# LayerNorm statistics and normalisation of a retention kernel: variance taken around the mean, and both tiles of a pair normalised on VectorE

## What is computed

```python
xn = _layernorm(x, axis=-1)                      # (x - mean) / sqrt(var + eps), over 1024
Q, K, V = xn@Wq+bq, xn@Wk+bk, xn@Wv+bv           # 16 heads of 64
retained = ((Q@K.T)/8 * decay_mask) @ V          # per head, decay 0.99**(i-j) for j <= i
s = (layernorm(retained)*gamma+beta) * sigmoid(xn@Wg+bg) @ Wo + bo
g = silu(gelu(xn@w1+b1) @ w2 + b2)
x = x + s * g
```

## Time and profile before

| | |
|---|---|
| median of two runs | 1882.03 us (1881.09 and 1882.97) |
| the profiled execution | 1881.47 us |
| its slowest core (core 1) | span 1879.9 us |
| spans of all cores | 1870.0 to 1879.9 us |
| mean granted TensorE clock | 0.815 to 0.817 of full speed on every core |
| busy, core 1 | PE 1335.6 us (71%), DVE 450.6 us (24%), ACT 383.8 us (20%), POOL 146.4 us (8%) |

### The profile page before, as it was taken

One profiled execution on the slowest core, in us unless ns is written; L12 is line 12 of the kernel. 1 busy time (PEld: TensorE's weight loads), 2 busy tenths in 40 slices (PEclk: granted clock), 3 DMA queues, 4 the chain that ended last, 5 costly groups with the idle time before them and its releaser, 6 DMA issues.

```text
span 1879.9 us, 21563 instructions; the slowest of 8 cores (1870.0 to 1879.9 us)
## 1 busy us (share of the span) xinstructions
PE 1335.6 (71%) x7562; PEld 708.9 (38%) x7562; DVE 450.6 (24%) x1264; ACT 383.8 (20%) x758; POOL 146.4 (8%) x144
## 2 busy tenths in 40 slices
PE   0266386685736786668757767877569999999994
PEld 0022032352322332333324323343136666666662
DVE  0413420133302522332324233242401011110011
ACT  1443203112012012021120120201012222221221
POOL 0000000000100100100100001001101122211222
PEclk9987598686865867768758767787679999999997
DMA  7201203399950000000000000004250121111110
GB/s 144 85 29 66 68 0 67 75 126 113 119 83 23 0 23 23 12 12 23 23 23 1 24 0 1 23 1 157 79 202 12 57 68 68 46 37 54 68 68 34
DMA packets 15905, 100.46 MB, mean 53 GB/s; under 512 B 3253, under 2 KB 3638, under 8 KB 11830
## 3 DMA queue, kind: packets, MB, share of 16 engines
q0 software_dynamic: 6144, 44.06, 13.6%
q1 hardware_dynamic: 9510, 46.62, 7.6%
q10 hardware_dynamic: 144, 8.39, 1.2%
HBM read 109.56 MB, written 33.55 MB: 76 GB/s over the span
## 4 chain that ended last, share of the span: by engine, by line
PE 63%; DVE 10%; DMA 9%; ACT 8%; issue 7%; POOL 2%; DVEq 0%; ACTq 0%; SPq 0%; POOLq 0%
PE pY L1043 12%; PE pH L1019 9%; PE pPJ L527 6%; PE pM L829 5%; PE pPJ L489 4%; DMA xg<-xpre 3%; PE pS L756 3%; PE pPJ L506 3%; PE pPJ L564 3%; DMA s_scr<-WB 3%; PE pLATE L663 2%; ACT xnb L358 2%; PE pRT L608 2%; PE pRT L622 2%; PE pSCB L581 2%
## 5 line engine op out<-in xcount | busy, mean ns | idle before, releaser
L1019 PE MATMUL pH<-xnT,WB 128*128 128x256 bf16 x2048 | 229.5, 274 | 11.7 <-ACT hT L1029 10.8
L1043 PE MATMUL pY<-WB,hT 128*128 128x512 bf16 x1024 | 226.2, 382 | 13.7 <-DMA WB<-w2b 13.7
L1019 PEld LDWEIGHTS pH<-xnT,WB 128*128 128x128 bf16 x2048 | 200.2, 98 | 42.6 <-issue 16.9
L756 PE MATMUL pS<-WB 128*128 128x512 bf16 x256 | 103.6, 526 | 120.0 <-POOL WB L746 66.5
L1043 PEld LDWEIGHTS pY<-WB,hT 128*128 128x128 bf16 x1024 | 100.8, 98 | 133.2 <-issue 17.2
L1029 ACT ACTIVATE hT<-pH,b1Ts 128x256 bf16<-128x256 f32 x256 | 99.7, 480 | 223.5 <-PE pH L1019 223.4
L1073 DVE SCALAR_TENSOR_TENSOR xg<-pY,xg 128x1024 f32<-128x1024 f32 x16 | 19.6, 1224 | 470.1 <-ACT xg L1070 428.1
L527 PE MATMUL pPJ<-xnT,WB 128*128 128x256 bf16 x1024 | 122.8, 283 | 12.5 <-DVE WB L518 12.3
L806 PE MATMUL pMR<-WB,cpreB 128*1 128x512 bf16 x48 | 23.9, 600 | 150.7 <-DVE WB L430 94.8
L593 DVE TENSOR_TENSOR WB<-pSCB,maskS 128x256 bf16<-128x256 f32 x128 | 54.3, 424 | 302.3 <-PE pSCA L587 296.3
L527 PEld LDWEIGHTS pPJ<-xnT,WB 128*128 128x128 bf16 x1024 | 96.8, 101 | 40.3 <-issue 16.5
(11 more groups left out here) (133 smaller groups left out, 1470.5 us busy)
## 6 DMA issues: line engine op xcount, KB each, us to landing
xg<-xpre SPq DMA_DIRECT2D x12, 1024.0 KB, 4.9
xg<-xseg SPq DMA_DIRECT2D x8, 1024.0 KB, 4.8
w1b<-w POOLq DMA_DIRECT2D x1, 8192.0 KB, 108.2
w2b<-w POOLq DMA_DIRECT2D x1, 8192.0 KB, 182.4
s_scr<-WB POOLq DMA_DIRECT2D x16, 512.0 KB, 3.0
xg<-xseg SPq DMA_DIRECT2D x16, 512.0 KB, 5.0
sld<-s_scr SPq DMA_DIRECT2D x16, 512.0 KB, 3.7
out<-sld POOLq DMA_DIRECT2D x16, 512.0 KB, 3.0
```

Of the source, the lines that this page charges most:

```text
L756: A("tensor", lambda e, it=it, dt=dt, ns=ns: e.matmul(pS[:, :], AsS[:, GRP * dt + 128 * it:GRP * dt + 128 * it + 128], WoS(1024 * dt + 512 ...
L1019: A("tensor", lambda e, dht=dht, dm=dm, sub=sub, pH=pH, gc=gc: e.matmul(pH[:, 256 * sub:256 * sub + 256], w1S(4096 * dm + 128 * dht, 128), ...
L1043: A("tensor", lambda e, lt=lt, dht=dht, ns=ns, it=it, pY=pY, half=half: e.matmul(pY[:, 512 * ns:512 * ns + 512], hT[:, 256 * lt + 128 * it ...
```

## The change

- `ln_stats` gets the negative mean between its two ACT passes: Copy with sum on ACT, then `nmu` for this one column on DVE, then Square with sum on ACT with `nmu` as its bias. What is summed is the squared distance from the mean.
- `ln_nr` loses the mean, its square, and the subtraction; mean, scale and eps become one operation. It has 16 operations instead of 19.
- `ln_finish` has one form: the DVE operation over the tile, for both tiles. The product `nbc` and the ACT operation L440 are gone.

The loops and stages that call the helpers are as before. The core of the diff (where lines are left out, lists of names for the waits are written differently):

```diff
             A("scalar", lambda e: e.activation(
                 xnb[:, :], xbuf[:, :], AF.Copy,
                 accum_out=nsum[:, cs[0]:cs[1]]),
               reads=[xtok], writes=["b.xnb", "b.nsum.%d" % sx])
-            A("scalar", lambda e: e.activation(
-                xnb[:, :], xbuf[:, :], AF.Square,
-                accum_out=v1c[:, cs[0]:cs[1]]),
-              reads=[xtok], writes=["b.xnb", "b.v1c.%d" % sx])
...
             A("vector", lambda e: e.tensor_scalar(
                 nmu[:, cs[0]:cs[1]], nsum[:, cs[0]:cs[1]], -1.0 / DM, None,
                 ALU.mult),
-              reads=_sxs("b.nsum", c0, ncols), writes=rm)
-            A("vector", lambda e: e.tensor_tensor(
-                nrT[:, cs[0]:cs[1]], nmu[:, cs[0]:cs[1]], nmu[:, cs[0]:cs[1]],
-                ALU.mult), reads=rm, writes=rt)
-            A("vector", lambda e: e.scalar_tensor_tensor(
-                vpe[:, cs[0]:cs[1]], v1c[:, cs[0]:cs[1]], 1.0 / DM,
-                nrT[:, cs[0]:cs[1]], ALU.mult, ALU.subtract),
-              reads=_sxs("b.v1c", c0, ncols) + rt, writes=rv)
+              reads=["b.nsum.%d" % sx], writes=["b.nmu.%d" % sx])
+            A("scalar", lambda e: e.activation(
+                xnb[:, :], xbuf[:, :], AF.Square, bias=nmu[:, cs[0]:cs[1]],
+                accum_out=v1c[:, cs[0]:cs[1]]),
+              reads=[xtok, "b.nmu.%d" % sx], writes=["b.xnb", "b.v1c.%d" % sx])
+
+        def ln_nr(c0, ncols):
+            cs = (c0, c0 + ncols)
+            sx = c0 // 2
             A("vector", lambda e: e.tensor_scalar(
-                vpe[:, cs[0]:cs[1]], vpe[:, cs[0]:cs[1]], EPS, None, ALU.add),
-              reads=rv, writes=rv)
+                vpe[:, cs[0]:cs[1]], v1c[:, cs[0]:cs[1]], 1.0 / DM, EPS,
+                ALU.mult, ALU.add),
+              reads=["b.v1c.%d" % sx], writes=["b.vpe.%d" % sx])
...
-            if eng == "vector":
-                A("vector", lambda e, rstd_ap=rstd_ap: e.tensor_scalar(
-                    out_ap, xbuf[:, :], nmu[:, cs[0]:cs[1]],
-                    rstd_ap[:, cs[0]:cs[1]], ALU.add, ALU.mult),
-                  reads=[xtok, "b.nmu.%d" % sx, rstd_tok] + list(extra),
-                  writes=[out_tok])
-                return
-            A("vector", lambda e, rstd_ap=rstd_ap: e.tensor_tensor(
-                nbc[:, cs[0]:cs[1]], nmu[:, cs[0]:cs[1]], rstd_ap[:, cs[0]:cs[1]],
-                ALU.mult),
-              reads=["b.nmu.%d" % sx, rstd_tok], writes=["b.nbc.%d" % sx])
-            A("scalar", lambda e, rstd_ap=rstd_ap: e.activation(
-                out_ap, xbuf[:, :], AF.Identity, bias=nbc[:, cs[0]:cs[1]],
-                scale=rstd_ap[:, cs[0]:cs[1]]),
-              reads=[xtok, "b.nbc.%d" % sx, rstd_tok] + list(extra),
+            A("vector", lambda e: e.tensor_scalar(
+                out_ap, xbuf[:, :], nmu[:, cs[0]:cs[1]], rstd_ap[:, cs[0]:cs[1]],
+                ALU.add, ALU.mult),
+              reads=[xtok, "b.nmu.%d" % sx, rstd_tok] + list(extra),
               writes=[out_tok])
...
-                    ln_finish(xb, xtok, t, xnb[:, :], "b.xnb",
-                              eng=("vector" if t == 0 else "scalar"))
+                    ln_finish(xb, xtok, t, xnb[:, :], "b.xnb")
...
-                                  scale_col=(cpreS[:, jt:jt + 1], "r.cpre"),
-                                  eng=("vector" if t2 == 0 else "scalar"))
+                                  scale_col=(cpreS[:, jt:jt + 1], "r.cpre"))
```

More of the change, by code:

```diff
@@ L289, in build_nc @@
         nrT = SB("nrT", [128, 4], F32)
-        nbc = SB("nbc", [128, 4], F32)
     if True:
@@ L392, in ln_nr @@
                 1, None, ALU.logical_shift_right),
-              reads=rv, writes=rn)
+              reads=["b.vpe.%d" % sx], writes=["b.nrY.%d" % sx])
             A("vector", lambda e: e.tensor_scalar(
@@ L396, in ln_nr @@
                 -1, None, ALU.bitwise_xor),
-              reads=rn, writes=rn)
+              reads=["b.nrY.%d" % sx], writes=["b.nrY.%d" % sx])
             A("vector", lambda e: e.tensor_scalar(
@@ L404, in ln_nr, with ln_finish @@
                     nrT[:, cs[0]:cs[1]], nrY[:, cs[0]:cs[1]], nrY[:, cs[0]:cs[1]],
-                    ALU.mult), reads=rn, writes=rt)
+                    ALU.mult), reads=["b.nrY.%d" % sx], writes=["b.nrT.%d" % sx])
                 A("vector", lambda e: e.tensor_tensor(
                     nrT[:, cs[0]:cs[1]], nrT[:, cs[0]:cs[1]], vpe[:, cs[0]:cs[1]],
-                    ALU.mult), reads=rt + rv, writes=rt)
+                    ALU.mult),
+                  reads=["b.nrT.%d" % sx, "b.vpe.%d" % sx],
+                  writes=["b.nrT.%d" % sx])
                 A("vector", lambda e: e.tensor_scalar(
                     nrT[:, cs[0]:cs[1]], nrT[:, cs[0]:cs[1]], -0.5, 1.5,
-                    ALU.mult, ALU.add), reads=rt, writes=rt)
+                    ALU.mult, ALU.add),
+                  reads=["b.nrT.%d" % sx], writes=["b.nrT.%d" % sx])
                 A("vector", lambda e: e.tensor_tensor(
                     nrY[:, cs[0]:cs[1]], nrY[:, cs[0]:cs[1]], nrT[:, cs[0]:cs[1]],
-                    ALU.mult), reads=rn + rt, writes=rn)
-        def ln_finish(xbuf, xtok, col, out_ap, out_tok, scale_col=None,
-                      extra=(), eng="scalar"):
+                    ALU.mult),
+                  reads=["b.nrY.%d" % sx, "b.nrT.%d" % sx],
+                  writes=["b.nrY.%d" % sx])
+        def ln_finish(xbuf, xtok, col, out_ap, out_tok, scale_col=None, extra=()):
             cs = (col, col + 1)
```

## The result

The changed kernel takes 1917.2 us (median), the kernel before 1882.3 us. The ratio is 1.018, 95% interval 1.016 to 1.020: it is slower by 1.8%, clear of zero, but less than the 2% from which a change counts as slower here. 1931 us were forecast, with a range from 1919 to 1942.

The account below looks back on a forecast made before the run. A chain of waits, with no engine full, was taken to set the prefix's pace. Prefix +49.7, groups 0 and 1 +1.8 and groups 3 to 7 -2.1 us gave +49.4 on 1881.47: 1931 us, range 1919 to 1942.

Parts of the forecast that it names:

- the large term: Prefix loop: DVE's new mean waits for ACT's Copy and holds the earlier pair's work and next load; +4.95 us a cycle.
- Rival A: Prefix: DVE isn't held, ACT leaves the release of the loads, 8.8 us a pair instead of 12.06; 1850 us, chance 0.04.
- Rival B: Group 2: PE's 28.64 us wait for a store shrinks by what the prefix grows; 1902 us, chance 0.10.
- Rival C: Gram blocks begin at the lower clock or DVE pays extra hand-overs, 10 to 15 us added; 1943 us, chance 0.08.
- Part 1 and 2: Prefix: the mean's trip over DVE between the ACT passes, and its place in DVE's queue; +49.7 us for the prefix.
- the last two groups: Main stage groups 0 and 1, where the first mean in group 1 stands behind DVE copy L915; +1.8 us together.
- step 1: Start of the prefix, pairs 0 and 1 both already loaded: next load issued at 58.6 against 54.51 us; +4.1 us.
- the eight steps with the full price: Prefix steps 2 to 8 and 10, each with the whole cycle growth: 8 x 4.95 = 39.6 us.
- step 9: Prefix behind the second Gram block, both kernels starting at 193.31: load issued at 203.1 against 202.01 us; +1.1 us.
- groups 0 and 1: First main-stage groups: group 0 gains 0.4 us, group 1's Square and second Copy come 3.0 us later; together +1.8 us.
- Part 4: Tile 1 normalised on DVE in stageE: -0.90 us there, -0.4 us net each, -2.1 us over groups 3 to 7.
- the bias: Per-partition bias operand of the Square pass: 0.09 us taken, bounds 0 and 0.17, moving the prefix 1.2 us either way.

Follow-up runs that it names:

- e4: The changed kernel with the statistics of pair k written behind the root, normalisation and load of the earlier pair in the prefix loop: 1866.3 us, ratio 0.991.
- e9: The changed kernel with the mean on POOL instead of DVE and the Wk and Wv transfers issued ahead of everything on POOL's queue: 1857.6 us, ratio 0.989.
- e3: The kernel before with only tile 1's normalisation moved to DVE, in the prefix and stageE, statistics as they were: 1833.7 us, ratio 0.974.
- e5: The changed kernel with the mean operation on POOL instead of DVE, nothing else edited: 1830.0 us, ratio 0.973.
- e10: e3 with the Wk and Wv transfers issued behind the first copy of the first Gram block: 1813.4 us, ratio 0.966 against the kernel before.

## Why the prediction missed

**What was right.** The mechanism of the large term. The mean stands ahead of the earlier pair's root in DVE's queue, the root and two normalisations come after the landing instead of before, and the load behind them. e4 shows it by the order alone, e9 by the engine of the mean alone. Rival A's mechanism, that ACT's leave from the release would gain some 30 us, is real but is in e3, not in the change: its price, 8.8 us a pair, came out as about 7.5 and 10 in turn. The cycle that both A and the forecast started from, 12.06 us, was a long one; it does no harm to the forecast, which needs only the 4.95 us by which the cycle grows. Rival B fell: the chain's store took 31.14 us on core 1 against 28.64, so it gave nothing back. Its second half, "a part of such a return, of 12 us or more from any source", is what came about, from the clock and not from the store. Rival C fell too; the second Gram block took 28.85 us on core 3, the first 29.38.

**Part 1 and 2, +49.7 us forecast.** Together with the last two groups 51.5 were forecast and 48.9 measured. The stretch was put at 11.08 us and took 10.85. The term that was mis-sized is the 0.27 us between the second mean and `ln_nr`: the first operation of `ln_nr` doesn't depend on that mean and started 0.07 us behind it (84.86 to 84.93). At eight cycles this is 1.6 us of the 2.6 missed. By steps, as the mean of the cores: step 1 cost 3.8 us (forecast 4.1), the eight steps with the full price 37.6 (39.6), step 9 1.1 (1.1), and what follows up to the end of the prefix 5.9 (4.9 + 1.8); the first load landed 0.5 us later. The 1.8 us for groups 0 and 1 holds a slip: 3.0 - 0.27 - 0.9 is 1.8 for group 1 alone, and with the 0.4 us that group 0 gains the sum is 1.4.

**Part 4, -2.1 us forecast for the main stage, -11.5 measured: the step that failed.** `stageE` itself came out near what was worked out: from the first Copy to the first matmul of `stageS` it took 15.95 us (756.52 to 772.47, core 1) against 16.65 before, so -0.70 us where -0.4 was forecast. The part from the first transpose gave the 0.90 us; the part before it cost 0.18 us (10.77 to 10.95) instead of 0.49. The forecast then took M1 and S at their old times, as PE work that the change doesn't touch. Their work was the same, their clock was not: -7.0 and -4.3 us. The prediction named "a shift of the clock's phases against the eight groups" as "another few us" of its range and put nothing for it into the sum, though the chain of before (core 1) already held the evidence, the same 128 matmuls of L527 at 14.32 us in one group and 15.95 in the next:

```profile
631.92 14.32 PE pPJ L527 x128
...
758.26 15.95 PE pPJ L527 x128
```

Six of seven M1 parts of core 1 had at least one fall, so there was something to win. Had the spread between 36.4 and 39.7 us in seven parts (seven at 36.4 are 12.7 us below the mean of 267.5, seven at 39.7 are 10.4 above it) been taken as the bounds of an unknown cost, as was done for the bias, the range would have reached down to about 1910 us: 1931 less 12, and less the 4 and 5 us for the bias and the loads, and the chance of "within 2%" would have had to be well above 0.13. Which way the shift would go was not worked out from the trace of before, and no run here shows that it could be.

In sum, 48.9 - 11.5 - 1.7 gives +35.7 us for the mean core; the medians of the slowest core lie 34.9 us apart. The 1.7 us of the last stage were not followed up.

## What to carry to other kernels

When a helper that ran on one engine gets an operation on a second, look up what is written behind each of its calls on that second engine: in a hand-pipelined loop the new operation waits for this step's data and holds up the last step's work, and its own 0.15 us say little of the price (4.7 us a cycle here). Change the order of writing together with the helper, or give the operation to an engine with nothing that waits behind it (POOL in e5 and e9). And where PE has short gaps, treat the granted clock of the stretches behind the edit as an unknown with bounds from the trace of before, not as a constant.

## What the hardware showed that was not expected

- The granted clock fell or stayed with the same matmuls: M1 took 36.4, 38.1 or 39.7 us, and four unused operations of 0.16 us in a stage some 25 us earlier moved the sum of seven from 260.5 to 271.3 us.
- A mean on POOL (a tensor_scalar over one column) took 0.21 us where DVE took 0.15, and its hand-over to ACT 0.46 us against 0.35: for a one-column value POOL is nearly as good as DVE. Where it ran beside DVE's operation over a tile, it took 0.52 to 0.76 us (six times in e5, cores 0 and 1, and e9, core 1).
- With 4 MB of weights issued at the start, the first 1 MB load landed at 40.7 us (e3, core 1), without them at 15.7 (e10). 23 of these 25 us lay in the wait for a transfer of 12 KB ahead of it on the queue (26.8 us, e3); two transfers moved gave them back.
